# Decoder layer, cross attention: the gate's high and low columns in one weight, its matmuls in two slots, the experts two slots sooner

## What is computed

```python
def _L0_ffn_ref(tokens, gate_w, w0, b0, w1, b1):
    logits = jnp.einsum('bsd,de->bse', tokens, gate_w)
    weights = jax.nn.softmax(logits, axis=-1)
    topk_w, topk_idx = jax.lax.top_k(weights, 2)
    ...
    e0 = jax.nn.silu(x @ w0.T + b0)
    e1 = jax.nn.silu(x @ w1.T + b1)
    m0 = (fidx[:, 0:1] == 0).astype(x.dtype)
    m1 = (fidx[:, 1:2] == 1).astype(x.dtype)
    out = e0 * fw[:, 0:1] * m0 + e1 * fw[:, 1:2] * m1
```

## Time and profile before

| | |
|---|---|
| median of 3 runs | 1775.47 us (1770.29 to 1775.82) |
| span of the profiled execution | 1773.4 us |
| TensorE busy | 1681.7 us, 95% |
| VectorE busy | 1254.6 us, 71% |
| ScalarE busy | 974.2 us, 55% |
| GpSimd busy | 1161.8 us, 66% |
| TensorE on the chain that ended last | 68% |

### The profile page before, as it was taken

One profiled execution on the slowest core, in us unless ns is written; L12 is line 12 of the kernel. 1 busy time (PEld: TensorE's weight loads), 2 busy tenths in 40 slices (PEclk: granted clock), 3 DMA queues, 4 the chain that ended last, 5 costly groups with the idle time before them and its releaser, 6 DMA issues.

```text
span 1773.4 us, 30895 instructions
## 1 busy us (share of the span) xinstructions
PE 1681.7 (95%) x10626; PEld 1111.0 (63%) x10626; DVE 1254.6 (71%) x2785; ACT 974.2 (55%) x1939; POOL 1161.8 (66%) x964
## 2 busy tenths in 40 slices
PE   5999999999999989999998999999999999999998
PEld 4766666666666547877863556566565656656566
DVE  5677777777777666767876776877778686777745
ACT  4555555555555443433445565656666665666554
POOL 2556556556555554744565977878788786878874
PEclk9999999999999989999998999999999999999999
DMA  6556555555555464576625543535344354534210
GB/s 199 147 149 168 145 152 156 153 156 165 141 153 153 122 194 152 181 219 185 193 66 155 144 115 88 139 90 155 91 114 114 82 138 99 144 93 108 63 42 31
DMA packets 167273, 237.29 MB, mean 134 GB/s; under 512 B 22087, under 2 KB 73287, under 8 KB 167117
## 3 DMA queue, kind: packets, MB, share of 16 engines
q1 hardware_dynamic: 167116, 235.31, 48.2%
HBM read 91.57 MB, written 41.94 MB: 75 GB/s over the span
## 4 chain that ended last, share of the span: by engine, by line
PE 68%; DVE 12%; POOL 8%; DMA 4%; issue 4%; ACT 2%; SPq 1%; POOLq 0%; DVEq 0%; ACTq 0%
PE bank L1652 9%; POOL cross_added L1974 7%; PE bank L201 5%; PE bank L202 5%; PE bank L203 5%; DVE bank L585 5%; PE bank L1522 5%; PE bank L1490 5%; PE bank L1461 5%; PE bank L369 4%; PE bank L305 4%; PE bank L356 3%; DVE bank L548 2%; PE bank L1558 2%; PE bank L329 2%
## 5 line engine op out<-in xcount | busy, mean ns | idle before, releaser
L1471 DVE TENSOR_REDUCE cross_negmax<-bank 128x1 f32<-128x512 f32 x512 | 338.7, 674 | 149.8 <-PE bank L1461 147.2
L1738 ACT ACTIVATE cpt<-bank 128x512 f32<-128x512 f32 x512 | 297.7, 595 | 143.6 <-PE bank L1490 140.1
L548 DVE CUSTOM_DVE_ANT_0 bank<-bank,future 128x128 f32<-128x128 f32 (+3 forms) x512 | 243.0, 488 | 177.8 <-PE bank L356 177.7
L430 ACT ACTIVATE pt<-bank 128x256 f32<-128x256 f32 (+3 forms) x512 | 217.5, 444 | 260.2 <-PE bank L305 256.1
L1974 POOL TENSOR_TENSOR cross_added<-cross_added,cpt 128x2048 f32<-128x2048 f32 x61 | 280.0, 4591 | 11.5 <-ACT cpt L1738 11.0
L618 POOL TENSOR_SCALAR_AFFINE_SELECT pt<-pt 128x512 f32<-128x512 f32 x128 | 81.1, 634 | 246.8 <-ACT pt L430 246.8
L1490 PE MATMUL bank<-cqk 98*128 98x512 f32 x512 | 227.4, 444 | 7.1 <-ACT cpt L1738 6.2
L1461 PE MATMUL bank<-cqk 96*128 96x512 f32 x512 | 212.5, 418 | 10.7 <-DVE cross_negmax L1471 8.6
L1974 POOL TENSOR_TENSOR cross_added<-cpt,cpt 128x2048 f32<-128x2048 f32 x32 | 146.6, 4581 | 84.0 <-ACT cpt L1738 84.0
L305 PE MATMUL bank<-qk 98*128 98x256 f32 (+2 forms) x512 | 180.6, 359 | 8.4 <-ACT pt L430 3.9
L356 PE MATMUL bank<-qk 96*128 96x256 f32 (+2 forms) x512 | 169.5, 335 | 4.4 <-DMA qk<-stage 4.4
(11 more groups left out here) (207 smaller groups left out, 3623.8 us busy)
## 6 DMA issues: line engine op xcount, KB each, us to landing
qk<-stage SPq DMA_DIRECT2D x384, 128.0 KB, 2.3
cqk<-cstage SPq DMA_DIRECT2D x384, 128.0 KB, 2.3
scratch_memory<-memory SPq DMA_DIRECT2D x32, 512.0 KB, 3.8
ma<-scratch_memory SPq DMA_DIRECT2D x32, 512.0 KB, 3.9
raw<-in_x_t SPq DMA_DIRECT2D x32, 256.0 KB, 2.9
v<-in_x SPq DMA_DIRECT2D x32, 256.0 KB, 3.2
scratch_y_ar<-y_ar SPq DMA_DIRECT2D x32, 256.0 KB, 2.4
my_ar<-scratch_y_ar SPq DMA_DIRECT2D x32, 256.0 KB, 4.6
```

Of the source, the lines that this page charges most:

```text
L548: dve.tensor_tensor_reduce(out=scores, in0=scores, in1=sh.future[:, SEQ - P * (qt + 1):SEQ], scale=-1.0, scalar=-NEG, op0=ALU.add, op1=ALU ...
L1471: dve.reduce_max(s.negmax[gm % 2][:, col:col + 1], max_bank(sh, m)[:, :], AX, negate=True).then_inc(s.dve_max, 1)
L1738: act.activation(s.pt[step % 3][:, j, :], sh.bank[2 + n % 2][:, :], ACT.Exp, scale=SCALE_CROSS).then_inc(s.act_exp, 1)
```

## The change

It puts the gate's high and low columns side by side in one weight of 16 columns, so that one matmul does high x high (rows 0 to 7) and low x high (rows 8 to 15); the third product, high x low, is added to rows 0 to 7. Eight matmuls instead of twelve stand in slots 37 and 38 instead of 37 to 40. The copy takes 16 rows. The transposes of the logits become f32 matmuls with `parts`, two 8 x 8 unit matrices on top of each other, which transpose and add both halves; `parts` is made once by an addition on VectorE in the memory phase. `LOGITS` and `EXPERT` and all slots of ln3 and of the store move two slots ahead.

```diff
+        self.gate = sb("gate_hi_lo", [P, GROUPS, 2 * EXPERTS], F32R)
+        self.gate_hi, self.gate_lo = self.gate[:, :, 0:EXPERTS], self.gate[:, :, EXPERTS:2 * EXPERTS]
...
+    both = sh.ident[0:2 * EXPERTS, 0:EXPERTS], sh.ident[0:2 * EXPERTS, EXPERTS:2 * EXPERTS]
+    dve.tensor_tensor(third.parts[:, :], both[0], both[1], ALU.add).then_inc(cw.dve_small, 1)
...
-GATE, LOGITS, EXPERT = 37, 42, 44
+GATE, LOGITS, EXPERT = 37, 40, 42
...
-STATS3, FACTORS3, APPLY3, STORE = (58, 64, 68, 76), (59, 65, 69, 78), (66, 71, 73, 81), (67, 72, 74, 82)
+STATS3, FACTORS3, APPLY3, STORE = (56, 62, 66, 74), (57, 63, 67, 76), (64, 69, 71, 79), (65, 70, 72, 80)
...
-    if GATE <= slot < GATE + GROUPS:
-        c = slot - GATE
+    if slot == GATE:
         pe.wait_ge(s.dve_x2t, TILES * (b + 1))
-        done = triple(pe, sh.bank[6][0:EXPERTS, :], (cw.gate_hi[:, c, :], cw.gate_lo[:, c, :]),
-                      (s.x2t_hi[:, c, :], s.x2t_lo[:, c, :]), c == 0, c == GROUPS - 1)
-        if c == GROUPS - 1:
-            done.then_inc(s.pe_gate, 1)
+        for c in range(GROUPS):
+            pe.matmul(sh.bank[6][0:2 * EXPERTS, :], cw.gate[:, c, :], s.x2t_hi[:, c, :], start=(c == 0), stop=False,
+                      skip_group_check=True)
+    if slot == GATE + 1:
+        for c in range(GROUPS):
+            done = pe.matmul(sh.bank[6][0:EXPERTS, :], cw.gate_hi[:, c, :], s.x2t_lo[:, c, :], start=False,
+                             stop=(c == GROUPS - 1), skip_group_check=True)
+        done.then_inc(s.pe_gate, 1)
     if slot == LOGITS:
         pe.wait_ge(s.act_lt, b + 1)
         for k in range(TILES):
-            done = pe.transpose(sh.bank[7][:, k * EXPERTS:(k + 1) * EXPERTS], s.x1t[0:EXPERTS, tile_of(k)],
-                                sh.ident[0:EXPERTS, 0:EXPERTS])
+            done = pe.matmul(sh.bank[7][:, k * EXPERTS:(k + 1) * EXPERTS], s.x1t[0:2 * EXPERTS, tile_of(k)],
+                             s.parts[:, :], start=True, stop=True)
...
-        act.activation(s.x1t[0:EXPERTS, :], sh.bank[6][0:EXPERTS, :], ACT.Copy).then_inc(s.act_lt, 1)
+        act.activation(s.x1t[0:2 * EXPERTS, :], sh.bank[6][0:2 * EXPERTS, :], ACT.Copy).then_inc(s.act_lt, 1)
```

More of the change, by code:

```diff
@@ L732, in __init__ @@
         self.a = sb("a", [P, P])
-        self.gate_hi, self.gate_lo = (sb(f"gate_{part}", [P, GROUPS, EXPERTS], F32R) for part in ("hi", "lo"))
+        self.gate = sb("gate_hi_lo", [P, GROUPS, 2 * EXPERTS], F32R)
+        self.gate_hi, self.gate_lo = self.gate[:, :, 0:EXPERTS], self.gate[:, :, EXPERTS:2 * EXPERTS]
         self.gate_raw = sb("gate_raw", [P, GROUPS, EXPERTS])
@@ L1098, in memory_round_vector @@
     if i == SMALL + 3:
-        memory_small_weights(dve, s, cw)
+        memory_small_weights(dve, s, third, cw, sh)
     t = i - BEHIND
@@ L1113, in memory_folded, with memory_small_weights @@
     act.activation(cw.wo[:, c, :], sh.bank[6][:, :], ACT.Copy).then_inc(cw.act_fold, 1)
-def memory_small_weights(dve, s, cw):
+def memory_small_weights(dve, s, third, cw, sh):
     dve.wait_ge(cw.small_landed, 16 * 7)
[L1118 to L1121, removed]
+    both = sh.ident[0:2 * EXPERTS, 0:EXPERTS], sh.ident[0:2 * EXPERTS, EXPERTS:2 * EXPERTS]
+    dve.tensor_tensor(third.parts[:, :], both[0], both[1], ALU.add).then_inc(cw.dve_small, 1)
+    dve.tensor_copy(cw.gate_hi, cw.gate_raw[:, :, :]).then_inc(cw.dve_small, 1)
+    dve.wait_ge(cw.dve_small, 2)
+    dve.tensor_tensor(cw.gate_lo, cw.gate_raw[:, :, :], cw.gate_hi.bitcast(F32), ALU.subtract).then_inc(cw.dve_small, 1)
     dve.tensor_copy(cw.rows[:, :, :], s.rows_raw[:, :, :]).then_inc(cw.dve_small, 1)
-    dve.wait_ge(cw.dve_small, 3)
+    dve.wait_ge(cw.dve_small, 4)
     dve.tensor_tensor(cw.rows[32:33, :, :], s.rows_raw[32:33, :, :], cw.rows[32:33, :, :].bitcast(F32),
@@ L1312, in __init__ @@
         self.ln2, self.ln3 = TileNorm(nc, sb, sem, "ln2"), TileNorm(nc, sb, sem, "ln3")
+        self.parts = sb("gate_parts_sum", [2 * EXPERTS, EXPERTS])
         sb = Place(nc, STACKS, second.even)
@@ L1586, in cross_batch @@
                     pe.wait_ge(second.dve_s, NG)
-                    pe.wait_ge(cw.dve_small, 4)
+                    pe.wait_ge(cw.dve_small, 5)
             else:
@@ L1909, in cross_constants @@
 def cross_constants(pool, s, cw):
-    pool.wait_ge(cw.dve_small, 4)
+    pool.wait_ge(cw.dve_small, 5)
     ones_rows(pool, s.kq, s.pool_ones)
```

## The result

The changed kernel takes 1776.93 us (median of 20 runs, 1774.01 to 1780.37), the kernel before beside it 1771.12 us (20 runs, 1766.39 to 1776.57): ratio 1.0032 with the 95% interval [1.0023, 1.0041], that is +5.7 us with +4.1 to +7.3. The forecast was +3.2 us, 1775.47 to 1778.7. So the sign holds and the loss stays small, but the interval lies above +3.2 us, and it holds the forecast's own border between "no change" and "slower", +5.3 us. That the absolute time came within 1.8 us of 1778.7 is partly luck: the forecast started from a median of three runs, 1775.47 us, which was 4.35 us above that of twenty, and its difference was 2.5 us too small. The profiled executions differ by only 0.3 us.

The account below looks back on a forecast made before the run. TensorE sets the pace (196.9 of 200 us busy), each slot waiting on ScalarE and VectorE two slots back. Six batches +4.3, the seventh -0.51, the end -0.55: +3.2 us, 1775.47 to 1778.7 us; range 1771 to 1784.

Parts of the forecast that it names:

- 1, gate: Gate matmuls, twelve become eight: 0.93 us less per batch, with nothing for the wider weight.
- 2, logits: Logits' four transposes become eight f32 matmul records: 0.76 us instead of 0.34, +0.42 per batch (+0.34 to +0.91).
- 3, wait at slot 43: VectorE's gate operations ahead of the maximum of slot 41 make TensorE wait 0.16 us at slot 43.
- Part 4: Experts two slots sooner: ScalarE's exponential 66, behind the last tanh, delays slot 68's scores; +0.50 per batch (0 to 1.0).
- Part 5: VectorE's statistics, moved to slot 74, delay TensorE's maximum of slot 76: +0.67 per batch (0.3 to 0.9).
- Part 6: Slot 79: ScalarE's apply waits for GpSimd's factors, +0.81, coinciding with earlier delays, so it adds nothing, only just.
- rival B: Slower: GpSimd's late factors hold ScalarE at slot 79; 1781.3 us, or 1784.3 with half a microsecond more; chance 0.24.
- Part 7: Slot 86: a later TensorE no longer waits for ScalarE, held by ln2's factors at slot 84; -0.15 per batch.
- Part 8: GpSimd's addition of slot 63 stays covered by 2 us; SyncE's reordered stores and loads cause no delay.
- Part 9: Kernel's end: VectorE's last silu product leaves the chain of reciprocals that TensorE awaits; -0.55 us once.
- Rival A: Matmul savings win, queues have slack: 1771.4, or 1768.4 us without logits' cost; strong form 0.07, weak form with C 0.27.
- Rival C: Gate matmuls covered VectorE, so their saving is eaten, later waits absorb the moves: 1775 to 1776; 0.27 with weak A.

Follow-up runs that it names:

- e12: e10 with the last normalization's fourth tile two slots sooner, as in the changed kernel (statistics 74, factors 76, apply 79, store 80): ratio 1.0007 [0.9995, 1.0019].
- e8: Changed kernel with the fourth tile's statistics back at slot 76, factors at 76, apply and store still at 79 and 80: single execution, 1773.3 us beside 1772.57 of before.
- e3: Merged gate with f32 logits alone; logits, experts and ln3 in the slots of the kernel before: ratio 1.0013 [1.0002, 1.0023].
- e2: Changed kernel with the tanh of a batch's last expert unit one slot later on ScalarE (67 instead of 66): ratio 1.0036 [1.0025, 1.0047].
- e5: Changed kernel with ln3's third and fourth tiles back in the slots they had before: ratio 1.0004 [0.9989, 1.0018].
- e6: e5 with e2's later tanh of the last expert unit: ratio 1.0000 [0.9986, 1.0013].
- e1: Changed kernel with ln3's last tile (statistics, factors, apply, store) back at slots 76, 78, 81, 82: ratio 1.0015 [1.0003, 1.0028].
- e11: Kernel before with e10's order of transfers alone (second and third tile's stores at slots 74, 75, residual's first tile at 74): ratio 0.9990 [0.9977, 1.0003].
- e9: e6 with the second and third tile's stores at slots 74 and 75, issued behind the keys' load: ratio 0.9995 [0.9981, 1.0009].
- e10: e9 with the residual's first tile also loaded behind the keys, at slot 74 instead of 70: ratio 0.9986 [0.9974, 0.9998].
- e4: Kernel before with the moves alone: twelve old gate matmuls packed into slots 37 and 38, old transposes in slot 40: ratio 1.0051 [1.0038, 1.0064].

## Why the prediction was right where it was, and where not

| part | forecast per batch | measured | where |
|---|---|---|---|
| 1, gate | -0.93 | -0.93 | 4 x 0.23 |
| 2, logits | +0.42 | +0.64 | 0.98 for eight records |
| 3, wait at slot 43 | +0.2 (its text has 0.16) | 0 | part 2 takes its place |
| 1 to 3 together | -0.31 | -0.33 | position at the start of a window +1.76, less nine matmuls |
| 4, slot 68 | +0.50 | +0.52 | that +1.76 less 1.57 is +0.19 behind slot 4; 0.19 + 0.33 |
| 5, slots 76 and 78 | +0.67 | +0.67 | changed kernel: 0.80 - 0.13; e12 |
| 6, slot 79 | 0 | 0 | e8, four windows of six |
| 7, relief | -0.15 | -0.01 | -0.19 at slots 85, 86, +0.18 at 90, 91 |
| sum | +0.71 | +0.81 to 0.83 | six windows but for the last slot, 615.63 to 620.59 us; the rows above add up to 0.85 |
| 9, end | -0.55 | -0.63 | below |

**Parts 1 to 3.** Right as a sum, for the reason that the forecast gave: what the logits cost and what TensorE waits at slot 43 replace each other. The term mis-sized is part 2. It was put near the transposes of the earlier trace rows because both move eight columns, but the record of an f32 product took 0.12 us, in the middle between the transposes' 0.085 and the 0.157 of the earlier trace rows. What was not in the forecast is why the gate's saving survives at all: e3 shows that with the logits two slots later it does not. The place of the logits in VectorE's hole at slot 40 is worth 0.4 us a batch (e3's +0.22 against the changed kernel's 1.89 less nine matmuls, -0.20), and a count of matmuls doesn't show it.

The Trainium skill's rule on loads ("TensorE: Matmul & The Clock Gate", section "LDWEIGHTS (loading the stationary operand)") gave an estimated 0.85 us for the logits' eight loads; the trace has 0.96 for the load records and 0.98 to the next matmul. The Trainium skill's sustained rate in the section "Back-to-back issue gap" of that page would have let four matmuls save an estimated 0.52 us; the trace has 0.93.

**Part 4.** The size was right, the cause half told. The forecast named ScalarE's order with the tanh. e2 and e5 each take one suspect away and gain nothing, e6 takes both and gains 0.26. The statistics of the third tile on VectorE, moved to slot 66, were just as late; the text had worked through one engine of the two whose results TensorE waits for. What is left, 0.27, is the round through an exponential, in which no small operation stands any more in e6.

**Part 5.** Right in place and size, to 0.01 us, and shown by taking it out (e1) and by putting it alone (e12). Worked from rows of one engine that ran without a gap, it was the surest step.

**Part 6 and rival B.** ScalarE does wait for GpSimd, and in more windows than before: between 1000 and 1700 us there are 13 waits of ln2's and ln3's apply, 27.4 us in all, against 7 of 22.4. The wait before the apply was 2.09 us, where 3 to 4 was forecast, because the copy of the next residual's transposes comes before it. TensorE, later by parts 4 and 5, arrives at the same time, as the forecast had it. Rival B needed 0.5 us more on GpSimd, and that didn't come; its wait costs TensorE time only in the two windows of e8. The measured +5.7 us lies just above +5.3, where the forecast had only B, with 0.24; it got there by another way than B's.

**Part 7.** This step failed. The relief at slots 85 and 86 is there, -0.19, but slots 90 and 91 give it back, +0.18. What TensorE does at slot 91 is timed by VectorE's additions and statistics of ln2, and they don't come sooner because a wait at slot 86 is gone: its transposes wait 0.52 us for the addition in every window now, in before 0.24 to 0.39 in four of six. e3 and e11 show the same exchange the other way round: +0.07 and +0.09 at the first place, -0.08 and -0.10 at the second. Six times 0.15 is 0.9 us, and 3.2 + 0.9 is 4.1: close to what the traces show from the second window to the end, and the lower end of the interval. The rest, up to the ratio's 5.7 us, I can't place. The traces are one execution each, and single windows scatter by up to 1 us, so it may lie there or in the phases ahead. Two of the long windows can be named: in window 4 of the changed kernel the scores of slot 80 waited 0.61 us for the transfer of `cross_shift` (slot 79 took 2.03 us and not 1.26), in window 5 slot 78 took 1.62 us and not 0.83. But before has two such windows as well, slot 78 at 1.53 and 1.97.

**Part 8.** Right on GpSimd: its addition ends 1.9 to 2.0 us ahead of the sum matmuls of slot 68 (4.2 in before), where 2 were forecast. Half wrong in what it left out. SyncE's queue was checked for buffers and for issue time, and by both nothing is late. Not checked was how long a transfer takes among others: against its slot the keys' load is issued no later, but it lands 4.2 to 5.4 us after the issue in the changed kernel and 4.8 to 5.7 in e6, in before 3.5 to 4.3. In the changed kernel this lay under the loss at slot 76, which is why the sum held; it comes to light once that loss is mended (e1, e6, e8), and e9 shows that the second tile's store ahead of it decides.

**Part 9.** Right: the idle time of TensorE fell from 1.43 to 0.82. Against the sums' start (1717.65 in before, 1718.49 now) the output projection starts 0.63 us sooner.

**Rival A** fell with the waits of parts 4 and 5. **Rival C** is the mechanism of e3, though not of the change as it was made.

## What to carry to other kernels

When work of one engine is moved ahead in a hand-made order, list for every slot that becomes short what each of the other engines still has to do in it. Here three limits lay within 0.3 us of each other at slots 66 to 68, and removing the named one gave nothing. A move that squeezes slots also squeezes the transfers issued in them: keep the load that is needed first ahead of stores that nobody waits for, and ahead of a load that must itself wait in the same queue. That reordering cost nothing; in the kernel before it came out at 0.9990, in an interval that includes 1, and together with the mended change at 0.9986. A small gain by relief of a wait counts only if the next wait behind it has another cause.

## What the runs showed of the hardware

An f32 product of 16 x 128 by 16 x 8 is two records of 0.12 us each, 0.98 us for four products, against 0.34 us for four transposes of the same output: the transposes are one record each. A weight of 16 columns was no slower than one of 8.

A transfer's time depends on what is right ahead of it. Issued at the same place, the keys' 256 KB landed 5.1 us after the issue in e6 (4.8 to 5.7 in six windows), 3.6 with one store of 256 KB less ahead (e9, 3.57 to 3.74 in five windows, 4.34 in the other) and 2.7 with one load less again (e10, 2.60 to 2.69 in five windows, 3.38 in the other): about a microsecond or more for each transfer. In the stretch around the issue the DMA engines were at 92% in e6 and at 96% in e9, so their share tells nothing of it.

TensorE's granted clock fell now and then at slots 27 to 31 of a window, in none (e4) to three (e1, e12) of windows 1 to 7, and not always in the same ones. In e12, window 6:

```profile
1553.89 0.63 PE L1609 MATMUL bank<-ident,x 128*128 128x128 f32 x4 [0.52 <-DVE x L1844]
...
1555.80 0.73 PE L1464 MATMUL bank<-cqk 96*128 96x512 f32 x1 [0.57 <-DVE cross_negmax L1474]
1556.46 1.94 PE L1525 MATMUL bank<-cpt,cv 128*32 128x512 f32 x8
```

```profile
1555.00:1558.00 3.00, 2.43 (x11) 0.43 (x9) 2.82 (x6) 1.74 (x4) 2.67 (x6) 0.65 0.03 8
```

The mean of 0.65 is a stretch at 1.2 GHz among 2.4 GHz: the eight matmuls with the values take 1.94 us and not 1.06. TensorE had waited 0.52 and 0.57 us in two slots just before. In window 4 of the same execution it had waited 0.53 and 0.57 at the same place and kept its clock, so the waits alone don't decide. A window with such a fall lasted 0.8 to 2.4 us longer (e9: 104.59 against 103.75; e12: 105.30 and 105.41 against 104.44; e10: 106.15 against 103.77). Whether a kernel without these two waits would be steadier wasn't tried.
